# Tile 1's deviations by TensorE's products, and a repacked tail

## The reference

```python
# 1: normalized over channels, then a recurrence over the 32 image rows
fs = conv(ln_c(x), w_itos * mask) + b_itos              # taps: row above, row itself
pre = conv(h, w_stos) + b_stos + fs[row]                # 3 taps along the row
i, g, f, o = split(pre, 4)
c_new = sigmoid(f) * c + sigmoid(i) * tanh(g);  h_new = c * sigmoid(o)
x = x + h                                               # of all rows
# 2: each of 32 experts picks 8 of an image's 1024 tokens
probs = softmax(ln_t(t) @ gate_w.T + gate_b, over tokens);  topv, topi = top_k(probs, 8)
pooled = sum_k(ln_t(t)[topi] * topv)                    # (image, expert, 64)
hid = gelu([pooled, 1] @ weight1)                       # 65 -> 256
o = [hid, 1] @ weight2                                  # 257 -> 64
t[topi] += o * topv
```

## Time and profile before

| | us |
|---|---|
| median of 3 runs (203.98 to 205.28) | 205.27 |
| the profiled execution | 204.0 |
| its span | 202.2 |
| granted clock of TensorE, mean | 0.983 of full |

### The profile page before, as it was taken

The page is one execution under the profiler, slowest core; times in us unless marked ns, Lnnn a source line. Parts: engine busy times, 40 slices in busy tenths (PEclk is TensorE's granted clock), DMA queues, the critical chain, the costliest instruction groups (busy, mean ns, idle before and its releaser), DMA issues.

```text
span 202.2 us, 10852 instructions
## 1 busy us (share of the span) xinstructions
PE 178.2 (88%) x4675; PEld 146.5 (72%) x4675; DVE 165.6 (82%) x605; ACT 109.8 (54%) x265; POOL 125.9 (62%) x114
## 2 busy tenths in 40 slices
PE   0899995999989999999999999999988988998800
PEld 1688884988869987987988889788755767684200
DVE  0898797899999899899989978978989999246960
ACT  2554543775645566664666666666468796540000
POOL 4456259698997988989798799399168740000000
PEclk9999999999999999999999999999999999999985
DMA  5754332412423412333231351521550231000896
GB/s 122 169 116 112 79 85 57 109 55 78 89 76 89 110 53 61 99 66 107 63 107 44 82 140 38 138 59 53 144 122 0 80 98 38 6 3 24 239 356 216
DMA packets 29120, 19.12 MB, mean 95 GB/s; under 512 B 2464, under 2 KB 28048, under 8 KB 29072
## 3 DMA queue, kind: packets, MB, share of 16 engines
q1 hardware_dynamic: 27440, 15.87, 30.5%
q10 hardware_dynamic: 1632, 2.56, 4.1%
HBM read 14.12 MB, written 4.30 MB: 91 GB/s over the span
## 4 chain that ended last, share of the span: by engine, by line
PE 61%; DVE 21%; issue 6%; POOL 4%; DMA 2%; ACT 1%; SPq 0%; DVEq 0%; POOLq 0%
PE ps L947 40%; PE ps L938 10%; PE ps L1007 4%; DMA xc<-in_x 2%; DVE ps L715 2%; DVE tail_room L931 2%; DVE xtok L931 2%; DVE st L674 2%; DVE lg L872 2%; DVE x_split L867 2%; POOL r L404 2%; PE ps L1072 1%; DVE v L662 1%; POOL xc L382 1%; DVE cands L861 1%
## 5 line engine op out<-in xcount | busy, mean ns | idle before, releaser
L947 PE MATMUL ps<-x_split,w_hi 64*64 64x256 f16 x1000 | 49.9, 273 | 2.6 <-DVE fc L718 1.3
L947 PEld LDWEIGHTS ps<-x_split,w_hi 64*64 64x64 f16 x1000 | 25.1, 106 | 14.9 <-issue 8.1
L382 POOL TENSOR_TENSOR xc<-xc,h 128x256 f32<-128x256 f32 x31 | 22.7, 733 | 20.5 <-DVE h_lo L699 20.5
L715 DVE TENSOR_TENSOR ps<-sg_i,ps 64x256 f32<-64x256 f32 x62 | 26.7, 430 | 6.8 <-ACT ps L513 5.1
L947 PE MATMUL ps<-h_hi,w_hi 64*64 64x256 f16 x750 | 31.8, 271 | 0.0
L947 PE MATMUL ps<-h_lo,w_hi 64*64 64x256 f16 x750 | 31.8, 271 | 0.0
L947 PE MATMUL ps<-h_hi,w_lo 64*64 64x256 f16 x750 | 31.8, 271 | 0.0
L499 ACT ACTIVATE ps<-ps,bias 128x256 f32<-128x256 f32 x32 | 14.3, 447 | 30.1 <-PE ps L947 30.1
L947 PE MATMUL ps<-x_split,w_lo 64*64 64x256 f16 x500 | 24.5, 269 | 0.0
L938 PE MATMUL ps<-ident,xc 128*128 128x128 f32 x128 | 18.5, 288 | 6.7 <-DMA xc<-in_x 5.2
L674 DVE BATCH_NORM_STATS2 st<-ps 128x6 f32<-128x64 f32 x128 | 18.6, 217 | 5.7 <-PE ps L938 5.7
(11 more groups left out here) (130 smaller groups left out, 331.0 us busy)
## 6 DMA issues: line engine op xcount, KB each, us to landing
xc<-in_x SPq DMA_DIRECT2D x14, 256.0 KB, 3.7
rb_xr<-scratch SPq DMA_DIRECT2D x14, 256.0 KB, 4.3
w1s<-in_L_ffn_weight SPq DMA_DIRECT2D x8, 256.0 KB, 3.5
w2s<-in_L_ffn_weight SPq DMA_DIRECT2D x8, 256.0 KB, 3.6
rbf<-scratch SPq DMA_DIRECT2D x24, 64.0 KB, 2.3
out<-xtok SPq DMA_DIRECT2D x4, 256.0 KB, 5.2
out<-xtok ACTq DMA_DIRECT2D x4, 256.0 KB, 5.8
out<-tail_room SPq DMA_DIRECT2D x3, 256.0 KB, 4.4
```

Source lines behind the costliest of these rows:

```text
L382: p.tensor_tensor(here, here, h32[:, i % 2, :].rearrange("p (b w) -> p b w", w=W), ALU.add) \
L715: v.tensor_tensor(ps_ig[half(h), :], sg_i[half(1 - h), :], pre[G][half(1 - h), 0:COLS], ALU.mult) \
L947: ins = pe.matmul(pre[gate][to, 0:COLS], w[half(h), tap, C * GATE_ORDER[gate]:][:, 0:C], data[half(h)], start=first and m == 0, stop=s_don ...
```

## The change

**Tile 1's deviations.** `spread_r0(1)`, `turn_r0(1)` and `keep_r0t(1)` are gone. In their place PE makes the broadcast itself: `spread_r0_here(k)` multiplies a column of r0, repeated 64 times as weights, by 64 columns of the identity, 16 products for each half k of the tile's tokens, into bank 6. The first stands where `turn_r0(1)` stood, the second after F and G of step 1. ACT copies each half to `rb` (`keep_rb`), the first after `hi_part` of step 1, the second ahead of `hi_part` of step 2. `scale_rows(1, k)` waits for its own half, and both halves now stand ahead of `rsqrt0(2)` on POOL. The counts of the later tiles' semaphores drop by one tile.

**Tail.** `pool(2)` stands ahead of `turn_picks(3)`. The turned means go to two banks: ACT copies those of groups 0 to 2 once they are turned, DVE those of group 3. Two experts now share 32 rows: each takes 16 rows, the other's being zero in `pool_t`, and both are summed in one region. The first layer has as many products; GELU has two parts, turns are 8, copies to `hid_t` two. The bias of the first layer has 4 products instead of 8, and the last bias add four parts of half the size instead of two.

```diff
@@ -141,16 +141,18 @@
...
             [xtok[:, 2 + b, :, :].rearrange("p b c -> p (b c)") for b in range(4)]
-        hid = xtok[:, 0:2, :, :].rearrange("p a b c -> p (a b c)").rearrange("p (q h) -> p q h", h=H)
-        hid_t = rb_xr[:, :, :].rearrange("p a (q k j) -> p (a q) k j", k=2, j=128)
+        hid = xtok[:, 0:1, :, :].rearrange("p a b c -> p (a b c)").rearrange("p (a r h) -> p a r h", a=2, h=H)
+        hid_t = rb_xr[:, 0, :].rearrange("p (a r k n) -> p a r k n", a=2, r=2, k=2)
         pick_t = rb_xr[:, :, :].rearrange("p a (t e) -> p a t e", e=128)
-        pool_t = w_stack[:, :, :, :].rearrange("p a n k -> p (a n k)")[:, 0:HALF_E * E].rearrange("p (e i) -> p e i", i=E)
+        pool_t = w_stack[:, :, :, :].rearrange("p a n k -> p (a n k)")[:, 0:HALF_E * E]
         o_img = h32[:, :, :].rearrange("p a k -> p (a k)")
...
@@ -161,11 +163,21 @@
...
         IDLE_BANK = psum[2]
-        PT_BANK = psum[6]
-        HID_BANKS = psum[0:2] + psum[4:6]
-        HT_BANKS = psum[2:4] + psum[6:8]
+        PT_BANKS = psum[6:8]
+        HIDDEN = [pairs[k][:, :, 0:H] for k in (0, 2)]
+        HT_BANKS = psum[2], psum[7]
         O_BANKS, OT_BANKS, OB_BANK = psum[0:2], psum[4:6], psum[0]
...
+        def turned_pool(r, last):
+            cols = PT_BANKS[last][0:C, 0:128 if last else 128 * (NG - 1)]
+            return cols.rearrange("p (i r n j) -> p r n j i", r=2, n=4, j=QUAD)[:, r, :, :, :]
+        def pool_cols(r, last):
+            images = slice(QUAD * (NG - 1), B) if last else slice(0, QUAD * (NG - 1))
+            return pool_t[half(r), :].rearrange("p (n j s) -> p n j s", n=4, s=E)[:, :, :, images]
...
             def spread_r0(u):
-                q.wait_ge(s_r0_kept, u)
+                q.wait_ge(s_r0_kept, u - 1)
...
@@ -330,10 +344,10 @@
...
             q.dma_start(b2_rows[:, :], w2[:, H, :]).then_inc(s_gate_w_in, DMA)
-            for k in range(4):
-                q.dma_start(b1_rows[E * k:E * k + E // 4, :], w1[E // 4 * k:E // 4 * k + E // 4, C, :]).then_inc(s_b1_in, DMA)
+            for r in range(2):
+                q.dma_start(b1_rows[E * r:E * r + E // 4, :, :],
+                            w1[HALF_E * r:HALF_E * r + HALF_E, C, :].rearrange("(a n) h -> n a h", a=2)).then_inc(s_b1_in, DMA)
             load_x(3, (0, 1))
-            spread_r0(1)
...
@@ -383,7 +397,10 @@
...
             def scale_rows(u, k):
-                p.wait_ge(s_rb_in, 2 * DMA * u)
+                if u == 1:
+                    p.wait_ge(s_rb_kept, k + 1)
+                else:
+                    p.wait_ge(s_rb_in, 2 * DMA * (u - 1))
...
@@ -400,7 +417,8 @@
...
                 if u > 2:
-                    p.wait_ge(s_r0_turned, u - 2)
+                    p.wait_ge(s_r0_spread, 2)
+                    wait(p, s_r0_turned, u - 3)
                 p.tensor_tensor(r0[:, u % 2, :], v0[:, 3, :], pow_exp[:, :], ALU.pow).then_inc(s_r0, 1)
...
@@ -438,10 +456,10 @@
...
                     scale_rows(1, 0)
+                    scale_rows(1, 1)
                     rsqrt0(2)
+                    lo_of_x(1, 0)
                     residual(0, 2)
-                    lo_of_x(1, 0)
-                    scale_rows(1, 1)
                 elif t + 1 < NT:
...
@@ -503,10 +521,12 @@
...
                 a.activation(sg_i[:, :], pre[I][:, 0:COLS], ACT.Sigmoid, bias=bias[:, 0:1]).then_inc(s_sg_i, 1)
-                if n == 1:
-                    keep_r0t(1)
+                if n == 2:
+                    keep_rb(1)
                 a.wait_ge(s_h32, n + 1)
                 hi_part(par, 1 - par)
+                if n == 1:
+                    keep_rb(0)
                 if i == 0 and t > 1:
...
+            def keep_rb(k):
+                a.wait_ge(s_r0_spread, k + 1)
+                a.activation(rb[:, :, 2 * W * k:2 * W * k + 2 * W], ps_lg.rearrange("p (b t) -> p b t", b=NB), ACT.Copy) \
+                    .then_inc(s_rb_kept, 1)
             def keep_r0t(u):
-                a.wait_ge(s_r0_turned, u)
-                wait(a, s_r0_stored, DMA * (u - 2))
+                a.wait_ge(s_r0_turned, u - 1)
+                wait(a, s_r0_stored, DMA * (u - 3))
                 a.activation(r0t[:, u % 2, :], ps_r[0:B, 0:TOK], ACT.Copy).then_inc(s_r0_kept, 1)
...
@@ -635,13 +662,10 @@
...
             for r in range(2):
-                a.activation(pool_t[half(r), :, 0:B].rearrange("p (a n) i -> p a n i", a=2),
-                             PT_BANK[0:C, :].rearrange("p (i a r n) -> p r a n i", a=2, r=2, n=E // 4)[:, r, :, :, :],
-                             ACT.Copy).then_inc(s_pool_t, 1)
-            for k in range(4):
-                a.wait_ge(s_hidden, k + 1)
-                a.activation(hid[:, 2 * k:2 * k + 2, :].rearrange("p q h -> p (q h)"), HID_BANKS[k][:, :], ACT.Gelu) \
-                    .then_inc(s_gelu, 1)
+                a.activation(pool_cols(r, 0), turned_pool(r, 0), ACT.Copy).then_inc(s_pool_t, 1)
+            for n in range(2):
+                a.wait_ge(s_hidden, n + 1)
+                a.activation(hid[:, n, :, :], HIDDEN[n], ACT.Gelu).then_inc(s_gelu, 1)
             for m in range(2):
...
@@ -903,17 +927,21 @@
...
                                        pooled[:, g, :], ALU.mult, ALU.add).then_inc(s_centered, 1)
-            for k in range(4):
-                v.wait_ge(s_hid_turned, k + 1)
-                v.tensor_copy(hid_t[:, 2 * k:2 * k + 2, :, :].rearrange("p q k j -> p (q k j)"), HT_BANKS[k][:, :]) \
-                    .then_inc(s_hid_t, 1)
-            for m in range(2):
-                v.wait_ge(s_o_turned, m + 1)
-                experts = slice(HALF_E * m, HALF_E * m + HALF_E)
-                v.tensor_tensor(o_t[:, :, experts].rearrange("p i (q j) -> p i q j", j=QUAD),
-                                OT_BANKS[m][0:C, :].rearrange("p (q j i) -> p i q j", q=4, j=QUAD)[:, 0:B, :, :],
-                                b2[:, experts].rearrange("p (q j) -> p q j", j=QUAD).unsqueeze(1)
-                                .to_broadcast([C, B, 4, QUAD]), ALU.add).then_inc(s_o_t, 1)
+            v.wait_ge(s_pooled_turned, 2)
+            v.wait_ge(s_pool_room, 1)
+            for r in range(2):
+                v.tensor_copy(pool_cols(r, 1), turned_pool(r, 1)).then_inc(s_pool_t, 1)
+            for n in range(2):
+                v.wait_ge(s_hid_turned, n + 1)
+                v.tensor_copy(hid_t[:, n, :, :, :].rearrange("p r k n -> p (r k n)"), HT_BANKS[n][:, :]).then_inc(s_hid_t, 1)
+            for r in range(2):
+                v.wait_ge(s_o_turned, r + 1)
+                for m in range(2):
+                    experts = slice(HALF_E * r, HALF_E * r + HALF_E)
+                    v.tensor_tensor(o_t[:, :, experts].rearrange("p i (a m j) -> p m i a j", a=2, m=2)[:, m, :, :, :],
+                                    OT_BANKS[r][0:C, :].rearrange("p (a m j s i) -> p m s i a j", a=2, m=2, j=QUAD, s=2)[:, m, m, :, :, :],
+                                    b2[:, experts].rearrange("p (a m j) -> p m a j", a=2, m=2)[:, m, :, :].unsqueeze(1)
+                                    .to_broadcast([C, B, 2, QUAD]), ALU.add).then_inc(s_o_t, 1)
             v.wait_ge(s_o_blocks, 1)
...
@@ -982,6 +1010,17 @@
...
+            def spread_r0_here(k):
+                pe.wait_ge(s_r0, 3)
+                wait(pe, s_rb_kept, k)
+                for b in range(NB):
+                    for h in range(2):
+                        ins = pe.matmul(ps_lg[half(h), 2 * W * b:2 * W * b + 2 * W],
+                                        r0[:, 1, 2 * b + h:2 * b + h + 1].to_broadcast([128, C]),
+                                        ident[:, 2 * W * k:2 * W * k + 2 * W], start=True, stop=True)
...
@@ -1015,11 +1054,11 @@
...
                     pe.wait_ge(s_x_stats, 4)
-                    turn_r0(1)
+                    spread_r0_here(0)
...
@@ -1031,8 +1070,10 @@
...
                     turn_x1(t - 1)
+                if i == 1 and t == 0:
+                    spread_r0_here(1)
                 if i == 3 and t == 0:
-                    pe.wait_ge(s_r0_kept, 1)
+                    pe.wait_ge(s_rb_kept, 2)
                     pe.wait_ge(s_gate_centered, 4)
...
@@ -1165,60 +1206,60 @@
...
             pool(1)
+            pool(2)
             turn_picks(3)
-            pool(2)
             pool(3)
-            pe.wait_ge(s_b1_in, 4 * DMA)
+            pe.wait_ge(s_b1_in, 2 * DMA)
             pe.wait_ge(s_row_expert, 4)
-            def first_bias(m):
-                for k in range(4):
-                    pe.matmul(HID_BANKS[k][:, H * m:H * m + H],
-                              row_expert[E * k:E * k + E // 4, QUAD * m:QUAD * m + QUAD, :].rearrange("p j i -> p (j i)"),
-                              b1_rows[E * k:E * k + E // 4, :], start=m == 0, stop=False)
+            def first_bias(n):
+                for r in range(2):
+                    pe.matmul(HIDDEN[n][:, r, :], row_expert[E * r:E * r + E // 4, :],
+                              b1_rows[E * r:E * r + E // 4, n, :], start=True, stop=False)
...
```

(111 more changed lines are left out.)

5 lines of the change are left out of this document (3 added, 2 removed).

## The result

| | before | after |
|---|---|---|
| median (lowest to highest) of 9 executions each, us | 204.69 (203.87 to 205.67) | 205.63 (205.20 to 206.86) |
| ratio to before, 95% interval | | 1.0057 (1.0031 to 1.0083) |
| profiled execution, us / its span, us | 204.0 / 202.2 | 205.37 / 203.6 |

The change costs 0.3 to 0.8% (+1.2 us by the ratio). That is inside the range and within 1%, but six times the +0.2 us of the forecast.

A forecast was written before the change was run, and what follows sets the result against it. PE was taken as the bound from 57 to 150 us, with 2.4 us of idling in the head. 0.45 + 0.5 - 0.45 - 0.3 = +0.2 us on the 205.27 median gave 205.4 us, range 203.3 to 206.6.

The forecast's parts named there:

- A group's price: Head, PE: the two added groups of 16 fp32 products take 1.05 us and 1.25 us.
- The collision: Head: DVE's `lo_part(2)` meets POOL's `scale_rows(1,1)` in SBUF, lasts over 1 us and ends at 28.9, not 28.05.
- 1.5 without the collision: Head: h of step 3 comes 2.17 us late, but 1.5 us if `lo_part(2)` does not meet POOL.
- h of step 3 and F, G of step 4: Head: h of step 3 at 32.69, not 30.52; PE starts F, G of step 4 at 35.3, not 34.85.
- +0.45 goes to the end: Head's term: +0.45 us (-0.4 to +2), carried undiminished to the end since PE is the bound from 57 us.
- The store and broadcast of tile 2: Head: broadcast at 35.8, not 34.89, POOL's next `scale_rows` at 40.7, not 39.80; 0.9 us, mostly hidden by POOL's idling.
- POOL late: Rival, chance 0.13: the 0.9 us at 39.80 isn't absorbed, r1 of tile 0 reaches PE late; +0.7 more, 206.1 us.
- `pool(2)` ahead, +0.5: Tail: 1.0 us of pooling against 0.47 of idling delays the turns; `pool(3)` runs alone after ACT's copies; +0.5 us.
- Means in two parts, -0.45: Tail: ACT copies three quarters early, DVE the rest in two copies of 0.17 us each; -0.45 us (-0.2 to -0.6).
- Two experts per 32 rows, -0.3: Tail, expert layers: fewer GELU parts, turns and copies give -0.5 us, the split last add +0.2; -0.3 us (-1.1 to +0.1).

The follow-up runs named there:

- Experiment 3: Changed kernel with `keep_rb(1)` behind `hi_part(2)` on ACT; ratio to the kernel before 1.0035 (1.001 to 1.006).
- experiment 2: `pool(2)` put back behind `turn_picks(3)`: in the changed kernel 1.006, in the old head with the new tail 0.9949, ratios to the kernel before.
- experiment 1: The change split, each half against the kernel before: only the head's edits, ratio 1.0073; only the tail's edits, ratio 0.995.
- experiment 5: Changed kernel, tile 2's store and broadcast ahead of tile 4's load: with two ACT moves 1.0075, alone 1.0051, with ACT moves and `pool(2)` behind `turn_picks(3)` 1.0029.
- 6: Old head with new tail, tile 2's broadcast held until h of step 4: ratio to before 0.9995 from four of twelve executions, against 0.995 without the delay.
- The head alone: Changed kernel with every edit behind step 31 undone; ratio to the kernel before 1.0073 (1.0044 to 1.0102).
- first kernel of experiment 5: Changed kernel with `keep_rb(1)` behind `hi_part(2)`, tile 2's copy ahead of `hi_part(3)`, tile 2's store and broadcast ahead of the load; ratio to before 1.0075.
- first kernel of experiment 2: Changed kernel with `pool(2)` behind `turn_picks(3)` again; ratio to the kernel before 1.006 (1.0039 to 1.0081).
- first ones of 4: Changed kernel with tile 2's copy of the turned deviations ahead of `hi_part(3)` on ACT; ratio to the kernel before 1.0042 (1.0014 to 1.007).

## Why the prediction was right, and where its sum was off

- **A group's price: right.** 1.15 us each (forecast 1.05 and 1.25), starts 20.21 and 23.08, O, I of step 2 at 24.16 (24.0).
- **The collision: right.** `lo_part(2)` 1.29 us long, to 29.0 (28.9). The Trainium skill's rule (SBUF — State Buffer, Who interferes with whom) holds for this pair, and not where POOL computes a power (last section). Experiment 3 separates the two, and the instruction takes 0.43 us. The forecast's "1.5 without the collision" does not follow from its own lines (28.05 + 3.79 is 31.84, 1.3 late); that experiment 3 measured 1.5 (32.19, less the 0.17 of its start) is luck.
- **h of step 3 and F, G of step 4: right.** 32.84 (32.69) and 35.47 (35.3). Less the 0.16 of the start, F, G of step 4 are 0.46 late; the forecast had 0.45.
- **"+0.45 goes to the end": wrong.** That what arrives goes on undiminished rested on the window from 57 us. Between 35 and 57 us PE idled 0.87 us in the kernel before, and in there the lateness was taken up: step 4's sigmoid(O) was not late at all, step 8's by 0.04.
- **The store and broadcast of tile 2: the term that failed**, put at nothing in the sum because POOL's later idling would hide 0.9 us. I moved the copy to 34.18 (measured 34.33) and took from tile 1 the 1.63 us between copy and broadcast. Tile 2's own rows stand in the earlier trace rows: copy 32.01, broadcast 34.89, 2.88 apart, since there a load shares the queue. With 2.88 the broadcast comes at 37.06 and, 4.91 us behind it as before (34.89 to 39.80), `scale_rows(2,0)` at 41.97. Measured: 37.07 and 42.03. The trace of before held the answer, and I read the wrong tile. My rival "POOL late", chance 0.13, is what the trace shows, with 2.2 us instead of 0.9 to absorb. I had named its marks: r1 of tile 0 late to PE, and DVE waiting behind POOL. The second is weak as a mark, since DVE met POOL twice at this place in the kernel before; now it is three times.
- **What came later: not in the sum.** Step 9 stands at +1.1, the last at +2.0. The rest arrives at step 22 (+0.6) and behind it, where a DVE instruction meets POOL for longer than before: L685 for 0.99 us at 106.75 against 0.41, behind which PE waits 0.43 us for `fc` at 110.67 (it did not before), and L723 for 1.34 at 124.15 against 1.13. I read this as the shifted phase between the engines; no run isolates it.
- **`pool(2)` ahead, +0.5: right, and 0.33 by experiment 2.** The turns started 0.36 later behind the pick than before, and `pool(3)` ran alone behind ACT's copies (174.83, after 0.80 of idling), as said.
- **Means in two parts, -0.45: -0.32.** ACT's part took 0.67 us, ahead of the last turn, and DVE's two copies 0.47 (forecast 0.34). With `pool(2)` behind the turns the first expert product came 6.26 us after the pick's start, before 6.58. Both terms were too large, by 0.17 and 0.13, so the first expert product kept its distance from the pick (+0.01), as the forecast had it (175.6 unchanged).
- **Two experts per 32 rows, -0.3: -0.6.** First expert product to second O copy: from 6.24 us to 5.49 (forecast 5.7). The forecast had added its own terms wrong: copy to 180.0 and 1.1 behind it make 181.1, not 181.3, and 181.1 was right. The adds took 1.01 us in all, where two took 0.42 each before, and from the second O copy to the output's first product it takes 0.14 us longer (2.49 against 2.35; forecast 0.2). Together that product stands 0.61 us nearer to the first expert product. By the ratios the tail gives 1.0 us, of which the traces show me 0.6; the interval of that ratio reaches down to 0.5 us.

The parts therefore: the tail -1.0 by experiment 1, where the forecast had -0.25, and the head +1.5, where it had +0.45. Two errors of opposite sign and a range of 3.3 us left the total inside. That the head loses the time is shown. That the late broadcast is the largest part of this loss is read from traces: from where the steps lose (step 9), from the one trace of experiment 5 where POOL is on time, and weakly from 6. No median bears it out: the kernels with a repaired order scatter over up to 4 us and gain nothing that can be told.

The traces show a second thing that takes time in the head: PE stops with no releaser. The head alone, timeline of PE:

```profile
19.81 0.28 PE L959 MATMUL ps<-h_hi,w_lo 64*64 64x256 f16 x4
...
20.64 0.42 PE L959 MATMUL ps<-h_hi,w_lo 64*64 64x256 f16 x8 [0.55 <-issue]
```

There the first group started at 21.32, 1.1 us later than in the kernel after; in the first kernel of experiment 5 the weight loads of the second group paused for 0.27 us, and the group took 1.55 us. Stops of PE of 0.33 to 0.63 us ahead of 57 us stand in five profiled executions with the new head: the head alone (206.66 us), the first kernel of experiment 2 (205.22), 3 (206.14), and the first ones of 4 (207.20) and 5 (207.40). They stand in none of the five others with the new head (203.39 to 205.37 us) and in none of the four with the old one. They come back at the same products: at about 51 us ahead of the last five `h_lo` products in three of these traces, at 56.4 ahead of the last one in two. In the traces the long executions are thus mostly the ones with such stops. What causes them, and whether the new instructions do, no run tells; nor how often they come in executions that were not profiled.

## What to carry to other kernels

When a step is moved, take the latency of its DMA chain from that step's own rows: the same store and broadcast took 1.63 us for one tile and 2.88 for the next, because a load was in the queue ahead of it. Bringing one transfer's work onto the compute engines can delay the next transfer of the same kind; follow the chain at least to the next tile. Measure parts of a bundled change apart: here one half gave 0.5% and the other took 0.7%. And look for the stretches where PE still idles behind an edit: what arrives late can be taken up there.
